# The last attention of a fused four-layer network: each query against the 64 keys of its own sequence, in smaller tiles of the array

## The reference

```python
S, B, H = hidden_states.shape            # 64, 128, 128
ln1 = _ln(hidden_states, ln1_weight, ln1_bias)
qkv = (ln1 @ qkv_weight.T).reshape(S, B, N_KV, (Q_PER_KV + 2) * HEAD_DIM)
q = qkv[..., :q_dim].reshape(S, B, N_HEADS, HEAD_DIM)           # 16 heads of 8
k = jnp.repeat(qkv[..., q_dim:q_dim + HEAD_DIM], Q_PER_KV, axis=2)
v = jnp.repeat(qkv[..., q_dim + HEAD_DIM:], Q_PER_KV, axis=2)   # 8 key/value heads
scores = jnp.einsum('sbhd,tbhd->bhst', q, k) / jnp.sqrt(jnp.float32(HEAD_DIM))
causal = jnp.tril(jnp.ones((S, S), bool))
attn = jax.nn.softmax(jnp.where(causal[None, None], scores, NEG), axis=-1)
attn_out = jnp.einsum('bhst,tbhd->sbhd', attn, v).reshape(S, B, H)
hidden_after_attn = hidden_states + attn_out @ proj_weight.T
```

## Time and profile before

| | us |
|---|---|
| median of 3 runs | 3462.65 (3456.01 to 3463.34) |
| the profiled execution: its time | 3456.26 |
| the profiled execution: its span | 3454.3 |
| TensorE busy in the span | 2847.6 (82%) |
| VectorE busy | 2137.1 (62%) |
| ScalarE busy | 1617.1 (47%) |
| GpSimd busy | 738.3 (21%) |

### The profile page before, as it was taken

The page is one execution under the profiler, slowest core; times in us unless marked ns, Lnnn a source line. Parts: engine busy times, 40 slices in busy tenths (PEclk is TensorE's granted clock), DMA queues, the critical chain, the costliest instruction groups (busy, mean ns, idle before and its releaser), DMA issues.

```text
span 3454.3 us, 123814 instructions
## 1 busy us (share of the span) xinstructions
PE 2847.6 (82%) x46829; PEld 1894.4 (55%) x46829; DVE 2137.1 (62%) x6318; ACT 1617.1 (47%) x3530; POOL 738.3 (21%) x999
## 2 busy tenths in 40 slices
PE   2999996699998997999989588885599994309994
PEld 1666665466664444666654366663366663307773
DVE  5666668777776775777752477777676765622223
ACT  3455555355554333555554255556555553403331
POOL 1233320233330000000000222221000000764553
PEclk9999996699999997999989799997699996559997
DMA  7233323122222000000000011112200002112214
GB/s 204 68 73 74 77 72 126 35 49 50 46 50 102 0 0 9 10 10 9 10 5 0 13 20 19 19 19 59 65 20 20 20 21 61 51 40 72 68 44 157
DMA packets 247824, 161.41 MB, mean 47 GB/s; under 512 B 135892, under 2 KB 221818, under 8 KB 246662
## 3 DMA queue, kind: packets, MB, share of 16 engines
q1 hardware_dynamic: 238470, 145.67, 16.4%
q0 software_dynamic: 9216, 13.88, 1.2%
HBM read 107.89 MB, written 56.82 MB: 48 GB/s over the span
## 4 chain that ended last, share of the span: by engine, by line
PE 64%; DVE 11%; issue 9%; SPq 5%; DMA 4%; POOL 4%; ACT 2%; ACTq 0%; DVEq 0%; POOLq 0%
PE ps L585 8%; PE ps L561 7%; PE ps L526 6%; PE ps L531 6%; PE ps L729 5%; PE ps L861 4%; PE ps L851 4%; POOL slots L1837 3%; PE ps L606 3%; DMA ffb<-b_dram 3%; DVE negmax L1305 3%; PE ps L506 2%; PE ps L571 2%; PE ps L554 2%; PE ps L498 2%
## 5 line engine op out<-in xcount | busy, mean ns | idle before, releaser
L1305 DVE TENSOR_REDUCE negmax<-ps 128x4 f32<-128x480 f32 (+1 forms) x1280 | 790.2, 659 | 478.6 <-PE ps L531 462.5
L939 ACT ACTIVATE ex<-ps 120x1024 f32<-120x1024 f32 (+1 forms) x640 | 656.0, 1027 | 70.9 <-PE ps L571 43.7
L561 PE MATMUL ps<-qk 32*120 32x128 f32 (+1 forms) x10240 | 451.4, 293 | 0.0
L1788 POOL TENSOR_SCALAR ffb<-ffb 128x480 bf16<-128x480 int32 (+1 forms) x128 | 232.4, 1816 | 662.0 <-PE ps L571 498.8
L561 PEld LDWEIGHTS ps<-qk 32*120 32x120 f32 (+1 forms) x10240 | 342.3, 185 | 21.9
L585 PE MATMUL ps<-ex,vpad 120*32 120x128 f32 (+1 forms) x10240 | 351.0, 278 | 1.6 <-DVE qk L1339 0.9
L585 PEld LDWEIGHTS ps<-ex,vpad 120*32 120x32 f32 (+1 forms) x10240 | 263.5, 110 | 55.4 <-issue 52.5
L1837 POOL DMA_INDIRECT slots<-xw,slot_of x128 | 132.0, 1032 | 603.0 <-DVEq L1683 561.6
L1286 DVE SCALAR_TENSOR_TENSOR qk<-ps,cols,cpack 128x480 f32<-128x480 f32 (+1 forms) x320 | 228.7, 715 | 39.7 <-ACT qk L918 39.7
L531 PE MATMUL ps<-qk 32*128 32x480 bf16 (+1 forms) x1280 | 251.2, 389 | 0.0
L924 ACT COPY mT<-ps 128x128 bf16<-128x128 bf16 x320 | 85.1, 266 | 346.2 <-PE ps L537 346.2
(11 more groups left out here) (242 smaller groups left out, 5113.2 us busy)
## 6 DMA issues: line engine op xcount, KB each, us to landing
ffb<-b_dram SPq DMA_DIRECT2D x256, 90.0 KB, 2.4
ctxT<-in_ctxT SPq DMA_DIRECT2D x256, 60.0 KB, 1.8
ffb<-in_mask SPq DMA_DIRECT2D x256, 60.0 KB, 2.0
slots<-xw SPq DMA_DIRECT2D x1, 10560.0 KB, 31.1
h_all<-slots SPq DMA_DIRECT2D x40, 264.0 KB, 2.8
z<-xw SPq DMA_DIRECT2D x1, 8192.0 KB, 24.6
b_dram<-bparts SPq DMA_DIRECT2D x64, 90.0 KB, 1.9
w_sb<-in_L_W SPq DMA_DIRECT2D x2, 2048.0 KB, 10.4
```

Source lines behind the costliest of these rows:

```text
L561: pe.matmul(bank(g)[:, k * P:(k + 1) * P], kblk[of, j, k * nk:(k + 1) * nk], qs[of, j, :], start=False, stop=False, skip_group_check=True)
L939: act.activation(ex[0:nk, j, c * 1024:(c + 1) * 1024], b_ps[c][0:nk, :], ACT.Exp).then_inc(S["e_ready"], 1)
L1305: dve.tensor_reduce(negmax[:, j, HG * g:HG * g + HG], a_ps[g % 2][:, 0:HG * nk].rearrange("p (a n) -> p a n", a=HG), AX.X, ALU.max, negate ...
L1788: pool.tensor_scalar(mask4[:, j, :, :].rearrange("p c n -> p (c n)"), raw[:, j, :, :].rearrange("p c n -> p (c n)"), 0.0, MASKED, ALU.is_e ...
```

## The change

Only attention 4 and `hidden_in` differ. A query's scores are made for the 64 keys of its own sequence alone, so everything that holds scores is half as wide: mask and scores by query are 256 instead of 512 columns, VectorE's reductions are 128x256, and the scores by key take half of each of four banks, with 64 partitions for one sequence and 64 for the other. The matmuls for the two sequences stand in tiles of 32 rows by 64 columns, twice as many, each with half the columns. The values stream 64 columns instead of 128. For that `vpad` holds, for each head, 16 columns for the first sequence's values and its one, and 16 for the second's (zero for the other sequence's keys): `values_in` writes it in two additions of 64 partitions, and `hidden_in` clears the buffer and writes the ones, once. `by_row` no longer transposes 256 columns in two transposes: eight matmuls against parts of the identity (64 columns each, in 128x64 tiles) pick for each sequence its own half of the result while turning it.

```diff
+                    if s == 4:
+                        scores_of_own(I, half)
+                        return
...
+                def scores_of_own(I, half):
+
+                    t, j = I
+                    for m in range(4):
+                        keys_of = slice(m // 2 * NB, m // 2 * NB + NB)
+                        for c in range(2):
+                            of = slice((2 * half + c) * 32, (2 * half + c) * 32 + 32)
+                            pe.matmul(a_ps[c][32 * m:32 * m + 32, 0:HG * NB], identb[of, of],
+                                      bc(bias4(j)[of, m, keys_of], HG), start=True, stop=False, skip_group_check=True)
+                    for a in range(2):
+                        own = slice(a * NB, a * NB + NB)
+                        for c in range(2):
+                            of = slice((2 * half + c) * 32, (2 * half + c) * 32 + 32)
+                            by_head = high(kblk[of, j, 0:HG * nk]).rearrange("p (h n) -> p h n", h=HG)
+                            mm = pe.matmul(a_ps[c][own, 0:HG * NB], high(qs[of, j, own]), by_head[:, :, own],
+                                           start=False, stop=True, skip_group_check=True)
+                            if a:
+                                mm.then_inc(S["a_ready"], 1)
...
+                def scores_by_own_key(I):
+
+                    t, j = I
+                    for m in range(4):
+                        own = slice(m // 2 * NB, m // 2 * NB + NB)
+                        for g in range(NG):
+                            of = slice(g * 32, g * 32 + 32)
+                            mine = ps[own, 2 + g, 0:HG * NB].rearrange("p (h n) -> p h n", h=HG)
+                            pe.matmul(mine[:, :, 32 * (m % 2):32 * (m % 2) + 32], bias4(j)[of, m, own], bc(identb[of, of], HG),
+                                      start=m % 2 == 0, stop=False, skip_group_check=True)
+                    for k in range(HG):
+                        if k == 2:
+                            turn_max(I)
+                        for a in range(2):
+                            own = slice(a * NB, a * NB + NB)
+                            for g in range(NG):
+                                of = slice(g * 32, g * 32 + 32)
+                                pe.matmul(ps[own, 2 + g, k * NB:(k + 1) * NB],
+                                          kblk[of, j, k * nk + a * NB:k * nk + a * NB + NB], qs[of, j, own],
+                                          start=False, stop=False, skip_group_check=True)
...
+                    if s == 4:
+                        for k in range(HG):
+                            for a in range(2):
+                                own = slice(a * NB, a * NB + NB)
+                                for g in range(NG):
+                                    of = slice(g * 32, g * 32 + 32)
+                                    mm = pe.matmul(ps[own, 2 + g, k * NB:(k + 1) * NB], selb[of, k, 0:NB], mT[of, j, own],
+                                                   start=False, stop=True, skip_group_check=True)
+                        mm.then_inc(S["b_ready"], 1)
+                        return
...
+                    if s == 4:
+                        for k in range(HG):
+                            for g in range(NG):
+                                of = slice(g * 32, g * 32 + 32)
+                                h = g * HG + k
+                                mm = pe.matmul(pv_ps[of, k * NB:(k + 1) * NB], vpad[:, j, 2 * (k % 2) + k // 2, of],
+                                               ex[:, j, h * NB:(h + 1) * NB], start=k == 0, stop=True,
+                                               skip_group_check=True)
+                        mm.then_inc(S["pv_ready"], 1)
+                        return
...
+                    if s == 4:
+                        for k in range(HG):
+                            for a in range(2):
+                                own = slice(a * NB, a * NB + NB)
+                                by_head = tr_ps[own, :].rearrange("p (b g k e) -> p b k g e", b=2, g=NG, k=2)
+                                by_group = by_head[:, k // 2, k % 2, :, :]
+                                mine = ident.rearrange("p (g a e) -> p g a e", g=NG, a=2)[:, :, a, :]
+                                mm = pe.matmul(by_group, pv_sb[:, j, k * NB:(k + 1) * NB], mine,
+                                               start=k == 0, stop=True, skip_group_check=True)
+                        mm.then_inc(S["tr_ready"], 1)
+                        return
...
+                    if s == 4:
+                        act.activation(ex[:, j, c * 512:(c + 1) * 512].rearrange("p (g n) -> p g n", g=2),
+                                       ps[:, 2 + 2 * c:4 + 2 * c, 0:HG * NB], ACT.Exp).then_inc(S["e_ready"], 1)
+                        return
...
+                    if s == 4:
+                        for a in range(2):
+                            own = slice(a * NB, a * NB + NB)
+                            mine = vpad[own, j, :, :].rearrange("p k (g m) -> p k g m", g=NG)
+                            ins = dve.tensor_tensor(mine[:, :, :, 2 * DH * a:2 * DH * a + DH],
+                                                    v_ps[own, :].rearrange("p (k g e) -> p k g e", k=HG, e=DH),
+                                                    rows[own, 0, :].rearrange("p (k g e) -> p k g e", k=HG, e=DH), ALU.add)
+                        ins.then_inc(S["vpad_ready"], 1)
+                        return
...
-                                          a_ps[g % 2][:, 0:HG * nk].rearrange("p (a n) -> p a n", a=HG),
+                                          a_ps[g % 2][:, 0:HG * wide].rearrange("p (a n) -> p a n", a=HG),
...
                 chain[0] += NB
                 dve.wait_ge(S["dve_step"], chain[0])
+                link(dve.memset(vpad[:], 0.0))
+                for a in range(2):
+                    own = vpad[a * NB:(a + 1) * NB, :, :, :].rearrange("p j k (g m) -> p (j k) g m", g=NG)
+                    dve.memset(own[:, :, :, (2 * a + 1) * DH:(2 * a + 1) * DH + 1], 1.0)
                 finish_stats(9)
```

More of the change, by code:

```diff
@@ L547, in scores_by_key @@
                         pe.wait_ge(S["e_ready"], nth("e_ready", s, i - 1, 2, 2))
+                    if s == 4:
+                        scores_by_own_key(I)
+                        return
                     parts = 3 if s == 0 else 1
@@ L1301, in maxima @@
                     t, j = I
+                    wide = NB if s == 4 else nk
                     i = num(I)
```

## The result

The changed kernel takes 3437.75 us (median of 5 runs, 3428.92 to 3441.82), the kernel before 3462.63 in the runs beside it. The ratio is 0.9934, with a 95% interval from 0.9915 to 0.9953: 23 us faster by the ratio. Forecast was slower, 3612 (3405 to 3640): the time lies on the wrong side of the kernel before, and inside the range only because the range was stretched to reach rival 1.

The account below looks back on a forecast made before the run. The last attention was taken as bound by a ring through TensorE and VectorE (6.41 us). Staying at 1.2 GHz adds 64 x (8.9 - 6.52) = 152 us, clearing 1.4: 3456.3 + 154 = 3610, given as 3612 (3405 to 3640).

Parts of the forecast that it names:

- rival 1: The last attention's clock rises within the first iterations and stays up: 3412 us, faster; chance 0.30.
- The clock: The last attention goes on at 1.2 GHz as it starts: 152 us more; chance of low clock to the end 0.50.
- 8.9 us for an iteration: Length of the changed last attention's iteration at 1.2 GHz, summed by pieces, against 6.52 us before.
- attention 2's first iteration: Earlier-trace comparison: 8.06 us without values or by_row, clock not raised; the changed loop was taken to resemble it.
- The ring: The last attention's longest chain at 2.4 GHz, values through additions, by_row, keys and scores back to values: 5.8 us.
- L498 to by_row: Ring leg from the query and key projections to by_row: 0.44 us.
- by_row to its reader: Ring leg of by_row's eight matmuls, 0.8 us, and 0.25 to its reader.
- keys to the scores: Ring leg from VectorE's key step to the first score matmul: 0.35 us.
- Reductions: VectorE's reductions in the last attention at 256 columns take 0.42 us each; 0.53 us less on the ring.
- the clearing: Clearing the value buffer once, on the path before the statistics: 1.4 us, between 0 and 3.
- rival 3: Half-wide tiles on the same rows run one after the other: 3437 us at 2.4 GHz, 3700 at 1.2; slow end 0.03.
- both TensorE and VectorE must shrink together: In the last attention's iteration, a gain on TensorE alone or VectorE alone counts in part only.

Follow-up runs that it names:

- e1: The changed kernel with TensorE held once between items 29 and 30 of 64 of the last attention, until GpSimd did 40 small clearings; 3469.72 us.
- e3: The changed kernel with the last attention's projected values moved to a free part of bank 3; 3411.54 us, ratio 0.9846.
- e7: e3 with TensorE's loop over the last attention cut from four items a turn to two; 3408.77 us, ratio 0.9856.
- e8: The changed kernel with TensorE's loop of two items a turn instead of four and nothing else; 3441.92 us, ratio 0.9942.
- e2: The kernel before the change with TensorE held once at the same item as in e1; 3490.47 us.
- e4: The kernel before with only the half-width scores by query and VectorE's maxima (256 columns) put in; 3431.09 us, ratio 0.9922.
- e6: The changed kernel with by_row's eight matmuls in the last attention issued twice; 3621.45 us.
- e9: e8 with by_row's eight matmuls in the last attention issued twice; 3476.84 us.
- e10: e7 with 26 matmuls that nothing reads, before the last attention's first item and in its waits; 3405.79 us, ratio 0.9844.

## Why the prediction was wrong

**The clock: the step that failed.** "I expect the changed stage to go on as it starts, at 1.2 GHz." The number in it was right (8.9 us for an iteration; e1 shows 8.96 and 8.92), and not by luck: its pieces add up to 8.81, not to the 8.9 written there, and e1's laps have each of the seven within 0.15 us, though its 0.213 us for a round of L585 is not what eight rounds in 1.87 us show (0.234). The inference was not right. It judged the changed loop nearer to attention 2's first iteration, which at 0.50 did about as much work for its time and did not raise the clock. But that iteration ran once, and the loop, as the prediction's own rival 1 said, has many tries. In every profile of the half-width loop that was not warmed beforehand the clock came up 12 to 33 us after the first turn of the maxima (after 15, e3 12, e7 23, e8 33), in e1's restart after two laps, where the old loop needed 9 (before) and one lap (e2). So the lighter loop does take longer, and how long differs from one kernel to the next; it does not stay down. In the changed kernel the rise at 2483.6 came 1.2 us behind the first iteration with values and by_row, and attention 2's at the end of its first such iteration: of its two rows the prediction leaned on the one without them. But e7 needed two such iterations, e8 three, and e1's restart two, so this does not say on which lap the clock rises; that stays open. The rule of the Trainium skill, TensorE: Matmul & The Clock Gate, Part 1, that sustained activity releases the clock, was set aside on the 9.52 of 10.00 us in the earlier trace rows; e1's restart, 18.18 busy of 18.70 us at 0.50 and 1.00 from then on, agrees with it in direction, and shows how long it can take.

**The ring: right in part, and mis-sized.** Rival 1 is what happened, "The clock rises within the first iterations and stays up", at 3412 us. Its ring, 5.8 us, is 6.03 measured. By pieces: values to the additions 0.75 (0.78 forecast), these to L498 0.83 (0.73), L498 to by_row 0.63 (0.44), by_row to its reader 0.74 (1.05), reciprocal to the keys' end 1.24 (1.24), keys to the scores 0.65 (0.35), scores to values 1.22 (1.22). Two terms were mis-sized for a reason: two projections cost 0.63 from their start to by_row's, and the scores came 0.30 later behind the keys than L526 behind L1286 in the earlier trace rows, since TensorE was still at its scores by key and L620 and did not wait for the keys. That leg is TensorE's own, as long in all as the way through VectorE that the sum took. by_row was sized too long; the 0.36 us that its sum gave to a change of tile shape no row shows, and L667 to L597 took 0.63 in all. One thing is left open on the ring: VectorE's additions (2610.36) stand directly behind its copy of the output (L1449), and the values' product (L641) ends 0.1 us before they start, so which of the two holds them no run tells. By the sum rival 1 gained 46 us; the longer ring takes 15 of them back (64 x 0.23), and the clock 8, in cold iterations and stops that the sum had at none. The 23 left are the stage's.

**The parts.** Reductions 0.419 us (0.42), values 0.58 at L641 to L544 (0.58), the clearing 0.91 (1.4). That 32x64 tiles on the same rows run side by side held: L606's 32 passes of 64 columns take 0.42 us from start to start (2607.20 to 2607.62), where before the change L561's 16 of 128 columns took 0.66 (2619.80 to 2620.46), and rival 3 falls. That both TensorE and VectorE must shrink together was said; no run shortens one of them alone, so it stays unproven. e4 shows a side that was missed: the two halved reductions and score steps alone gave 0.47 of the 0.49.

## What to carry over

Before a loop is forecast to stay at a low clock, ask how often it gets to try: a single cold lap proves little against 64. When work is taken from one engine, look for who now ends its waits; here the gain of half the change came only once the freed half banks were used to undo a shared bank (3437.75 to 3411.54 us). Count the instructions that unrolling and smaller tiles put into a loop, since past a point the loop's code is loaded anew in every turn: here 780 matmuls with as many weight loads stayed, and 844 with as many did not.

## What was not expected of the hardware

The loop whose code did not stay on the engine cost 127 more code packets of 16 KB and about 145 us (e6 against e9, 214 and 87 packets, 3621.45 and 3476.84 us, one run each). Part of that went through the clock, which fell in the stage again and again:

```profile
2515.00:3000.00 485.00, 396.22 (x10877) 294.14 (x10879) 203.41 (x621) 135.02 (x363) 0.00 (x0) 0.75 0.08 18
```

This is a window of e6; the mean clock is 0.75 where e9's stood at 1.00. What starts a fall of the clock stays open. In three kernels with the long loop it fell again within 24 us of its first rise, for 3.4 us in the changed kernel, 10.2 in e3 and 17.1 in e1 ahead of the pause, each time within 3 us of a stop of 0.8 to 1.4 us without any wait; but the changed kernel's and e3's first such stops, and one of 1.07 us in e10 (until 2485.52), were followed by none.
